# Edge stage of a graph network: TensorE's signals raised by a drain and a sequencer instruction instead of by the last matmul

## The chip, the core and the metric

The kernel runs on one core of one Trainium2 chip. The metric is device time in microseconds (us) for one execution of the whole program. Before the change it takes 3927.65 us (median of three runs, 3921.35 to 3943.58).

The engines are named as in the profile: PE (TensorE, matmuls), PEld (its weight loads), DVE (VectorE), ACT (ScalarE), POOL (GpSimd) and SP (SyncE). [...]

## The reference, cut to what matters

Four layers run one after the other on x of 8192 nodes by 128 features: a dense graph attention (`L0_gnn`), a mixture of four experts whose gates come from a sparse graph attention (`L0_ffn`), another dense graph attention (`L1_gnn`) and a second mixture of experts (`L1_ffn`). The change touches the second one alone:

```python
h = (x_flat @ W_gat).reshape(M, HEADS, NUM_EXPERTS)          # 4 heads, 4 experts
e = leaky_relu(a_src[src] + a_dst[dst], negative_slope=0.2)   # one row per edge
ee = exp(e - e_max[dst])
denom = segment_sum(ee, dst)
agg = segment_sum(h[src] * (ee / denom[dst])[:, :, None], dst)
...
for ei in range(NUM_EXPERTS):                                 # dense: every expert on every node
    hh = gelu(x @ W1[ei] + b1[ei])
    out = out + g[..., None] * (hh @ W2[ei] + b2[ei])
```

524288 edges are given, and a self loop is added for every node.

## The kernel before, in words

The stage is the block `edges` of the function `edge_gates` (from line 1023). It does two things at once: the sparse sums over the edges, and the four dense experts on all nodes. An earlier stage has sorted the edges into records, so that each of 128 partitions holds the edges of its own nodes.

**The loop.** Work goes in chunks of 16 columns of records (`CK = 16`). Four chunks (`RG = 4`, counted by `g`) make one round, and here there are five rounds: 20 chunks. In the first four rounds (`LEAD = 4`, so 16 chunks) every chunk also carries one slab of 512 nodes through the four experts. The last round has edges alone. Below, "the first 16 chunks" and "the last four chunks" mean these two loops.

**What one chunk does, by engine.**

- SP (line 1088) loads the records of a chunk into `RC[g]`, as soon as DVE has counted `gt_read` for the chunk four places earlier.
- POOL (line 1134) then issues 16 indirect DMAs, each of which gathers 128 rows of the table `tab` into `GT[g]`. Below, these 16 are called a burst.
- PE turns one-hot matrices (`look_up`, line 1362, two groups of eight transposes into `TB`, each raising `turned`), ACT copies them to `OHT` (line 1282), and PE multiplies them with `near` (line 1370, 16 matmuls into `LK`, raising `lk_ok`).
- DVE waits for `lk_ok` (line 1220), reduces `LK` (line 1221), forms the logits (lines 1223 to 1231), builds the one-hots of the next chunk (line 1152), waits for ACT's exponential (line 1287), multiplies (line 1238, after which it counts `gt_read`) and splits the values into three bf16 parts `VP` (to line 1244).
- PE scatters them (`scatter`, line 1380, 16 matmuls, raising `sc_ok`), and DVE adds the sums up (lines 1161 and 1162).
- For each expert e of the slab, PE runs `hidden` (line 1340: two matmuls of 512 columns in fp32, each recorded as two, raising `h_ok` after each), ACT applies gelu (line 1293, raising `hid_ok`), PE runs `output` (line 1348 for the bias, line 1351 for 8 matmuls, recorded as 16, raising `y_ok`), and ACT copies the result (line 1300, raising `y_used`) and sends it off (line 1303).

**The order on PE** is written out by hand: hidden(0), look_up, hidden(1), output(0), hidden(2), output(1), hidden(3), output(2), scatter, output(3). Each engine works through its own list in order, so an instruction that waits holds up all that stands behind it. Between engines there are only semaphores. A wait is followed by an increment of a semaphore `passed`, on which nobody waits; the two become one sequencer instruction.

**What PE signals, and how.** Five semaphores go from PE to the others: `h_ok` (8 per chunk of the first 16), `y_ok` (4), `turned` (2), `lk_ok` (1) and `sc_ok` (1), together 16. Each is raised by the last matmul of its group (`.then_inc`), on its completion. Signals of the sequencers, such as DVE's `gt_read`, `z_ok` and `vp_ok`, are raised by `sem_inc`, an instruction of the sequencer itself.

Of the kernel before, what the change touches and what calls it, by code (L numbers as in the profile page):

```python
# [18 lines left out]
P = 128  # L19
# [916 lines left out]
def edge_gates(nc, ident, rec, tab, tab_out, rows, ctl, repeat, b_gat, ln_gamma, ln_beta, G, XT, W1, b1, W2, b2, y, YB, y_in):  # L936
# [9 lines left out]
    NH = HE // NE  # L946
    T = N // P
    VW = NH + HE
    CK = 16
# [3 lines left out]
    D, HID = W1.shape[1], W1.shape[2]  # L953
    K = HID // P
    NG = N // BANK
    GQ = BANK // P
    NB2 = 3
    LEAD = NG // RG
    HK = CK // 2
    a_src, a_dst = rows[:, :, HE:HE + NH], rows[:, :, HE + NH:TW]  # L960
    assert HID == K * P and K == 2 and NE == 4 and RG == 4 and LEAD == 4
    with Phase(nc, "gat") as ph:
        near = ph.sbuf("near", [P, T, 3 * NH], BF16)
# [10 lines left out]
        with Phase(nc, "pre") as pp:  # L974
# [6 lines left out]
            dve_step, ext_ok, turned, diag_ok, all_ok = pp.sems("dve_step", "ext_ok", "turned", "diag_ok", "all_ok")  # L981
            with nc.Block() as block:
                @block.sync
                def _(sp):
                    sp.dma_start(RC[0][:], rv[:, 0:CK, :]).then_inc(rc_in[0], 16)
# [37 lines left out]
        with Phase(nc, "edges") as pr:  # L1023
            GT = [pr.sbuf(f"GT{k}", [P, CK, TW]) for k in range(RG)]
            node_no = pr.sbuf("node_no", [P, P])
            identB = pr.sbuf("identB", [P, P], BF16)
            OH = [pr.sbuf(f"OH{k}", [P, CK, P], BF16) for k in range(RG)]
            OHT = pr.sbuf("OHT", [P, CK, P], BF16)
            VP = pr.sbuf("VP", [P, CK, 3, VW], BF16)
# [18 lines left out]
            down = pr.sbuf("down", [P, NE, K, D])  # L1048
# [4 lines left out]
            HH = [[YB[0][:, b * K + k, :] for k in range(K)] for b in range(2)]  # L1053
            YS = [YB[1][:, e, :] for e in range(NE)]
            HP = pr.psum("hp", [P, K, BANK])
            YP = pr.psum("yp", [P, BANK])
            TB = [pr.psum(f"tb{h}", [P, HK * P], BF16) for h in range(2)]
            LK = pr.psum("lk", [P, BANK])
            OUT = [pr.psum(f"out{h}", [P, BANK]) for h in range(2)]
# [22 lines left out]
            with nc.Block() as block:  # L1082
# [250 lines left out]

                @block.tensor
                def _(pe):
                    def hidden(u, e):
                        for k in range(K):
                            pe.wait_ge(hid_ok, u * K + k + 1)
                            pe.sem_inc(passed, 1)
                            nc.tensor.matmul(HP[:, k, :], up[:, e, k * P:(k + 1) * P], XT[:, bass.ds(slab[0] * GQ, GQ), :],  # L1340
                                             start=True, stop=True).then_inc(h_ok, 1)

                    def output(u, e):
                        pe.wait_ge(hid_ok, u * K + 2 * K)
                        pe.sem_inc(passed, 1)
                        pe.wait_ge(y_used, u + 1)
                        pe.sem_inc(passed, 1)
                        nc.tensor.matmul(YP[:], oneB[0:NB2 * 32, :], b2s[0:NB2 * 32, e, :, :], start=True, stop=False)
                        for q in range(GQ):
                            for k in range(K):  # L1350
                                ins = nc.tensor.matmul(YP[:, q * D:(q + 1) * D], HH[e % 2][k][:, q * P:(q + 1) * P],  # L1351
                                                       down[:, e, k, :], start=False, stop=(q == GQ - 1 and k == K - 1))
                        ins.then_inc(y_ok, 1)

                    def look_up(k, g):
                        pe.wait_ge(oh_ok, k + 1)
                        pe.sem_inc(passed, 1)
                        for h in range(2):
                            pe.wait_ge(oht_ok, k * 2 + h + 1)
                            pe.sem_inc(passed, 1)  # L1360
                            for c in range(HK):
                                ins = nc.tensor.transpose(TB[h][:, c * P:(c + 1) * P], OH[g][:, h * HK + c, :], identB[:])
                            ins.then_inc(turned, 1)
                        pe.wait_ge(lk_read, k + 1)
                        pe.sem_inc(passed, 1)
                        for h in range(2):
                            pe.wait_ge(oht_ok, k * 2 + h + 3)
                            pe.sem_inc(passed, 1)
                            for c in range(h * HK, (h + 1) * HK):
                                ins = nc.tensor.matmul(LK[:, c * 3 * NH:(c + 1) * 3 * NH], OHT[:, c, :], near[:, g * CK + c, :], start=True, stop=True)  # L1370
                        ins.then_inc(lk_ok, 1)

                    def scatter(k, g):
                        pe.wait_ge(vp_ok, k + 1)
                        pe.sem_inc(passed, 1)
                        pe.wait_ge(acc_ok, k + 1)
                        pe.sem_inc(passed, 1)
                        for c in range(CK):
                            o = c % HK * 3 * VW
                            ins = nc.tensor.matmul(OUT[c // HK][:, o:o + 3 * VW], OH[g][:, c, :], VP[:, c, :, :].rearrange("p k v -> p (k v)"),  # L1380
                                                   start=True, stop=True)
                        ins.then_inc(sc_ok, 1)

                    rounds = rounds_of(pe)
                    pe.sem_inc(lk_ok, 1)
# [4 lines left out]
                    with pe.Fori(0, n) as l:  # L1390
                        off = begin(pe, l)
                        with pe.Fori(0, LEAD) as r:
                            for g in range(RG):
                                k, q = (off + r) * RG + g, r * RG + g
# [10 lines left out]
                        with pe.Fori(LEAD, rounds) as r:  # L1405
                            for g in range(RG):
                                k = (off + r) * RG + g
# [1482 lines left out]
```

## Time and profile before

| | us |
|---|---|
| median of three runs | 3927.65 |
| lowest, highest | 3921.35, 3943.58 |
| span of the profiled execution, first to last instruction | 3888.4 |
| median less span (start and end of the program, which the span leaves out) | 39.25 |
| edge stage, first 16 chunks (from the first `hidden` to the first matmul of the last round) | 617.6 |
| edge stage, last four chunks (to the last DVE sum) | 68.7 |

The page gives the times of one profiled execution. Its own time is not listed apart from the three; the span and the median stand 39.25 us apart. Matmul starts are recorded and their ends modelled. The name that the page gives as the releaser of a wait is inferred: where it names a transfer of an earlier stage (`sort_recs<-in_adj_dram`, `at_adj<-in_adj_dram`, `pj_Y<-in_x_dram`), the code at the waiting line says what is really waited for.

### The profile page before, as it was taken

The numbers are of one execution on the slowest core, as the hardware profiler recorded it, in microseconds if no ns is written. First come the engines' busy times: TensorE is split into PE (matmuls) and PEld (weight loads), VectorE is DVE, ScalarE is ACT, GpSimd is POOL, SyncE is SP. The second block draws the span as 40 slices with busy tenths as digits, with TensorE's granted clock in tenths as the row PEclk, the third lists the DMA queues.
The fourth block names the chain that finished last, engine by engine and source line by source line (L and its number), as shares of the span: only waits on it lengthen the run. The fifth ranks groups of instructions, "written<-read, shape, count | busy, mean of one in ns | idle before, by whom it ended". The sixth has DMA issues, their size and how long they took to land. (4 is left out here: it accounts for less than half of the span.)

```text
span 3888.4 us, 55206 instructions
## 1 busy us (share of the span) xinstructions
PE 2760.5 (71%) x16302; PEld 1676.9 (43%) x16302; DVE 2359.1 (61%) x4497; ACT 1367.3 (35%) x2278; POOL 1058.8 (27%) x1034
## 2 busy tenths in 40 slices
PE   0432127799999999994156566415899999959994
PEld 0432126644444444444044344315466566635662
DVE  9999798787878878876222222377544444343333
ACT  5310100077877878774033333214200011002221
POOL 0000100277777100000634444300012111123442
PEclk9999999999999999995577778655899999979997
DMA  5999790154645545431211112142333333314446
GB/s 203 349 383 410 303 410 22 48 194 175 218 157 189 185 168 217 154 136 44 28 39 36 33 36 38 27 163 100 96 109 108 109 105 107 104 66 129 130 126 187
DMA packets 233148, 567.74 MB, mean 146 GB/s; under 512 B 52065, under 2 KB 93384, under 8 KB 224446
## 3 DMA queue, kind: packets, MB, share of 16 engines
q1 hardware_dynamic: 145318, 375.39, 28.2%
q10 hardware_dynamic: 56152, 163.80, 11.3%
q0 software_dynamic: 31552, 27.13, 3.4%
q8 instruction: 46, 0.75, 0.1%
q14 instruction: 80, 0.66, 0.1%
HBM read 442.65 MB, written 125.39 MB: 146 GB/s over the span
## 5 line engine op out<-in xcount | busy, mean ns | idle before, releaser
L1777 PE MATMUL at_out<-at_pt,top_H 128*128 128x512 f32 x2048 | 932.0, 602 | 33.4 <-ACT at_agg L1629 29.8
L1619 ACT ACTIVATE at_rl<-at_qrow,at_less,at_steep 128x512 f32<-128x512 f32 x1024 | 742.2, 804 | 88.9 <-DVE at_pt L1705 45.4
L1705 DVE SCALAR_TENSOR_TENSOR at_pt<-at_rl,at_turned 128x1024 f32<-128x1024 f32 x512 | 626.5, 1224 | 157.2 <-PE at_out L1777 80.3
L1994 PE MATMUL at_out<-at_parts,at_a 128*128 128x387 bf16 x4096 | 688.2, 329 | 20.6 <-DVE at_parts L2067 15.7
L1777 PEld LDWEIGHTS at_out<-at_pt,top_H 128*128 128x128 f32 x2048 | 373.1, 190 | 437.8 <-issue 394.8
L1994 PEld LDWEIGHTS at_out<-at_parts,at_a 128*128 128x128 fp8e4 x4096 | 399.6, 98 | 296.1 <-issue 26.3
L896 POOL DMA_INDIRECT rec<-at_part x304 | 383.0, 1260 | 104.6 <-issue 89.0
L1134 POOL DMA_INDIRECT edges_GT<-tab,gat_RC x320 | 313.2, 979 | 335.2 <-DMA gat_RC<-rec 234.6
L1942 POOL DMA_INDIRECT slots<-at_Y,at_dest x128 | 123.3, 963 | 641.9 <-DVEq L2172 605.8
L1340 PE MATMUL edges_hp<-top_H,edges_up 128*128 x256 | 171.8, 803 | 148.7 <-issue 76.2
L645 PE MATMUL pack_bp<-top_weights,sort_recs 128*128 128x8 bf16 x1696 | 75.9, 170 | 234.7 <-DMA sort_recs<-in_adj_dram 234.7
L1221 DVE TENSOR_REDUCE edges_adv<-edges_lk 128x64 f32<-128x192 f32 x20 | 7.2, 358 | 349.1 <-DMA sort_recs<-in_adj_dram 345.1
L2445 PE MATMUL ex_hp<-ex_XS,ex_WB 128*128 128x512 f32 (+1 forms) x472 | 217.2, 597 | 1.8 <-DMA ex_WB<-wts 1.8
L2551 POOL DMA_INDIRECT y<-ex_YS,ex_to x156 | 153.3, 983 | 199.8 <-DVE ex_YS L2532 162.2
L2029 ACT ACTIVATE at_small<-at_small 128x4 f32<-128x4 f32 x16 | 3.3, 205 | 535.8 <-DVEq L2125 535.8
L2511 DVE TENSOR_TENSOR ex_HH<-ex_SU,ex_hp 128x512 f32<-128x512 f32 (+1 forms) x118 | 80.9, 686 | 162.2 <-ACT ex_SU L2489 121.5
L1293 ACT ACTIVATE f_YB<-edges_hp,edges_b1col 128x512 f32<-128x512 f32 x128 | 81.7, 684 | 251.6 <-DMA at_adj<-in_adj_dram 214.8
L645 PEld LDWEIGHTS pack_bp<-top_weights,sort_recs 128*128 128x128 fp8e4 x1696 | 61.8, 106 | 250.0 <-DMA sort_recs<-in_adj_dram 141.7
L1120 POOL IOTA edges_node_no<- 128x128 f32 x1 | 0.2, 238 | 574.0 <-POOLq L60 574.0
L1351 PEld LDWEIGHTS edges_yp<-edges_down,f_YB 128*128 128x128 f32 x1024 | 142.5, 214 | 30.8 <-issue 27.7
L2489 ACT ACTIVATE ex_SU<-ex_hp 128x512 f32<-128x512 f32 (+1 forms) x118 | 70.3, 595 | 235.1 <-PE ex_hp L2445 185.9
L1696 DVE TENSOR_SCALAR at_turned<-at_packed 128x512 uint16<-128x512 uint16 x520 | 148.0, 286 | 0.0
(543 smaller groups left out, 3745.2 us busy)
## 6 DMA issues: line engine op xcount, KB each, us to landing
sort_recs<-in_adj_dram SPq DMA_DIRECT2D x212, 512.0 KB, 8.9
at_adj<-in_adj_dram SPq DMA_DIRECT2D x192, 512.0 KB
adjT<-at_turned ACTq DMA_DIRECT2D x64, 1024.0 KB
at_a<-adjT SPq DMA_DIRECT2D x128, 512.0 KB
bucket_raw<-in_adj_dram ACTq DMA_DIRECT2D x120, 512.0 KB, 10.2
ex_WB<-wts SPq DMA_DIRECT2D x42, 533.0 KB
y<-f_YB ACTq DMA_DIRECT2D x64, 256.0 KB, 2.8
f_YB<-y SPq DMA_DIRECT2D x16, 1024.0 KB, 11.0
```

The source lines that it names most:

```text
L645: ins = nc.tensor.matmul(BP[:, u % 2, o:o + WORDS // 4], raw_bits[s % NR][:, k * P:(k + 1) * P, 0], weights[:], start=True, stop=True)
L896: pool.indirect_dma_start(rec, bass.IndirectOffsetOnAxis(ap=part[h][:, c, 2:3], axis=0), part[h][:, c, 0:2], None, bounds_check=LAST, oob_ ...
L1134: pool.indirect_dma_start(GT[g][:, c, :], None, tab, bass.IndirectOffsetOnAxis(ap=RC[g][:, c, 1:2], axis=0)).then_inc(gt_in[g], 16)
L1340: nc.tensor.matmul(HP[:, k, :], up[:, e, k * P:(k + 1) * P], XT[:, bass.ds(slab[0] * GQ, GQ), :], start=True, stop=True).then_inc(h_ok, 1)
L1351: ins = nc.tensor.matmul(YP[:, q * D:(q + 1) * D], HH[e % 2][k][:, q * P:(q + 1) * P], down[:, e, k, :], start=False, stop=(q == GQ - 1 an ...
L1619: ins = nc.scalar.activation(RL[v % NBUF][:, k, :], qrow[:], ACT.Relu, bias=less[:], scale=steep[:, u:u + 1])
L1696: ins = nc.vector.tensor_scalar(planes[m % 2][:, :, :, b, :], PK[:, m * JP:(m + 1) * JP, :].rearrange("p j (t w) -> p j t w", t=RT), b, 0x ...
L1705: nc.vector.scalar_tensor_tensor(out=PT[v % NBUF][:], in0=RL[v % NBUF][:], scalar=1.0, in1=AT[v // VP % 2][:, 2 * (v % VP):2 * (v % VP) + ...
L1777: ins = nc.tensor.matmul(OUT[:], H[:, u, :], PT[v % NBUF][:, k, :], start=(u == 0), stop=(u == T - 1))
L1994: ins = nc.tensor.matmul(OUT[:, g, x, 0:3 * D1], ones[c % NBUF][:, j, x * P:(x + 1) * P], parts[:, u].rearrange("p k d -> p (k d)"), start ...
L2445: ins = nc.tensor.matmul(HP[0:n, k, s, :], WB[b][:, w:w + n], XS[b][:], start=True, stop=True)
L2551: pool.indirect_dma_start(y, bass.IndirectOffsetOnAxis(ap=to[b][:, q:q + 1], axis=0), YS[b][:, q, :], None, bounds_check=2 * N - 1, oob_is ...
```

## The change

A helper `done` is added to the TensorE program of the block: it issues a drain, an instruction with which the sequencer waits until its engine has finished what was issued to it, and then a `sem_inc`. The five places that raised a semaphore with the last matmul of a group call it instead. No matmul, no wait and no other engine's program changes.

```diff
+                    def done(sem):
+                        nc.tensor.drain()
+                        pe.sem_inc(sem, 1)
+
                     def hidden(u, e):
                         for k in range(K):
                             pe.wait_ge(hid_ok, u * K + k + 1)
                             pe.sem_inc(passed, 1)
                             nc.tensor.matmul(HP[:, k, :], up[:, e, k * P:(k + 1) * P], XT[:, bass.ds(slab[0] * GQ, GQ), :],
-                                             start=True, stop=True).then_inc(h_ok, 1)
+                                             start=True, stop=True)
+                            done(h_ok)
...
-                        ins.then_inc(y_ok, 1)
+                        done(y_ok)
...
-                            ins.then_inc(turned, 1)
+                            done(turned)
...
-                        ins.then_inc(lk_ok, 1)
+                        done(lk_ok)
...
-                        ins.then_inc(sc_ok, 1)
+                        done(sc_ok)
```

## Rows read from the trace of the kernel before

**Rows 1.** The page: span, and TensorE's granted clock (tenths) in 40 slices.
```profile
span 3888.4 us, 55206 instructions
...
PEclk9999999999999999995577778655899999979997
```
**Rows 2.** Waits from 1868 to 2560: who waited for whom; total us, times, longest.
```profile
DVE edges_adv L1221 <- DMA sort_recs<-in_adj_dram: 345.1, 17, 53.5
POOL edges_GT L1134 <- DMA gat_RC<-rec: 234.6, 16, 17.5
...
DVE edges_adv L1221 <- PE edges_lk L1370: 4.0, 3, 1.3
```
**Rows 3.** Timeline of one chunk: start, us, engine, line, op, [idle before, releaser].
```profile
2208.04 1.88 PE L1340 MATMUL edges_hp<-top_H,edges_up 128*128 x4
...
2212.62 1.01 ACT L1282 COPY edges_OHT<-edges_tb 128x1024 bf16<-128x1024 bf16 x1
...
2214.70 1.01 ACT L1282 COPY edges_OHT<-edges_tb 128x1024 bf16<-128x1024 bf16 x1 [1.06 <-DMA pj_Y<-in_x_dram]
...
2215.86 0.36 PE L1370 MATMUL edges_lk<-gat_near,edges_OHT 128*128 128x12 bf16 x8 [1.74 <-ACT edges_OHT L1282]
...
2216.11 3.52 PE L1340 MATMUL edges_hp<-top_H,edges_up 128*128 x4
...
2219.69 1.95 PE L1351 MATMUL edges_yp<-edges_down,f_YB 128*128 128x128 f32 x16
...
2226.30 0.95 POOL L1134 DMA_INDIRECT edges_GT<-tab,gat_RC  x1 [0.30 <-issue]
2230.24 0.36 DVE L1221 TENSOR_REDUCE edges_adv<-edges_lk 128x64 f32<-128x192 f32 x1 [22.43 <-DMA sort_recs<-in_adj_dram]
2230.26 1.26 ACT L1293 ACTIVATE f_YB<-edges_hp,edges_b1col 128x512 f32<-128x512 f32 x2 [14.55 <-DMA at_adj<-in_adj_dram]
...
2231.09 3.75 PE L1340 MATMUL edges_hp<-top_H,edges_up 128*128 x4 [9.46 <-ACT f_YB L1293]
...
2244.27 1.02 PE L1340 MATMUL edges_hp<-top_H,edges_up 128*128 x2
```
**Rows 4.** Windows: stretch, length, busy of PE, PEld, DVE, ACT, POOL, granted clock.
```profile
1891.00:1895.00 4.00, 3.91 (x13) 1.69 (x14) 0.00 (x0) 0.00 (x0) 3.08 (x4) 0.50 0.13 9
1895.00:1901.80 6.80, 2.32 (x17) 2.00 (x16) 0.00 (x0) 0.00 (x0) 4.97 (x7) 1.00 0.11 9
```
**Rows 5.** Drains on PE's sequencer at a phase's end, with the matmuls before each.
```profile
2552.05 0.95 PE L1380 MATMUL edges_out<-edges_VP,edges_OH 128*128 128x60 bf16 x16 [8.70 <-DVEq L1245]
...
L1082 PEldq DRAIN  x1: 485/485/485, 2552.6 to 2552.6; - x1
...
3832.65 2.84 PE L2480 MATMUL ex_yp<-ex_WB,ex_HH 128*128 128x128 f32 x24
...
L2394 PEldq DRAIN  x1: 1968/1968/1968, 3833.6 to 3833.6; - x1
```
**Rows 6.** Lines by source: count, ns min/median/max, first to last start.
```profile
L1340 PE MATMUL edges_hp<-top_H,edges_up x256: 592/595/1217, 1868.9 to 2481.0; 128*128 x128
...
L1339 PEldq EVENT_SEMAPHORE  x128: 51/51/51, 1868.7 to 2479.1; - x128
```
**Rows 7.** Timeline: both ends of the first 16 chunks, and the look-up after them.
```profile
1868.94 3.78 PE L1340 MATMUL edges_hp<-top_H,edges_up 128*128 x4 [16.91 <-issue]
...
2486.51 1.06 PE L1362 MATMUL edges_tb<-edges_identB,edges_OH 128*128 128x128 bf16 x16
...
2493.34 0.36 PE L1370 MATMUL edges_lk<-gat_near,edges_OHT 128*128 128x12 bf16 x8 [1.96 <-issue]
...
2504.22 0.36 DVE L1221 TENSOR_REDUCE edges_adv<-edges_lk 128x64 f32<-128x192 f32 x1 [17.89 <-DMA sort_recs<-in_adj_dram]
```
**Rows 8.** Timeline, PE alone, in the first long burst.
```profile
1898.23 0.27 PE L1351 MATMUL edges_yp<-edges_down,f_YB 128*128 128x128 f32 x1 [1.45 <-issue]
1900.35 0.27 PE L1351 MATMUL edges_yp<-edges_down,f_YB 128*128 128x128 f32 x1 [1.84 <-issue]
1903.13 0.37 PE L1351 MATMUL edges_yp<-edges_down,f_YB 128*128 128x128 f32 x1 [2.52 <-issue]
```

More of the change, by code:

```diff
@@ L1350, in output @@
                             for k in range(K):
-                                ins = nc.tensor.matmul(YP[:, q * D:(q + 1) * D], HH[e % 2][k][:, q * P:(q + 1) * P],
-                                                       down[:, e, k, :], start=False, stop=(q == GQ - 1 and k == K - 1))
-                        ins.then_inc(y_ok, 1)
+                                nc.tensor.matmul(YP[:, q * D:(q + 1) * D], HH[e % 2][k][:, q * P:(q + 1) * P],
+                                                 down[:, e, k, :], start=False, stop=(q == GQ - 1 and k == K - 1))
+                        done(y_ok)
                     def look_up(k, g):
@@ L1361, in look_up @@
                             for c in range(HK):
-                                ins = nc.tensor.transpose(TB[h][:, c * P:(c + 1) * P], OH[g][:, h * HK + c, :], identB[:])
-                            ins.then_inc(turned, 1)
+                                nc.tensor.transpose(TB[h][:, c * P:(c + 1) * P], OH[g][:, h * HK + c, :], identB[:])
+                            done(turned)
                         pe.wait_ge(lk_read, k + 1)
@@ L1369, in look_up @@
                             for c in range(h * HK, (h + 1) * HK):
-                                ins = nc.tensor.matmul(LK[:, c * 3 * NH:(c + 1) * 3 * NH], OHT[:, c, :], near[:, g * CK + c, :], start=True, stop=True)
-                        ins.then_inc(lk_ok, 1)
+                                nc.tensor.matmul(LK[:, c * 3 * NH:(c + 1) * 3 * NH], OHT[:, c, :], near[:, g * CK + c, :], start=True, stop=True)
+                        done(lk_ok)
                     def scatter(k, g):
@@ L1379, in scatter @@
                             o = c % HK * 3 * VW
-                            ins = nc.tensor.matmul(OUT[c // HK][:, o:o + 3 * VW], OH[g][:, c, :], VP[:, c, :, :].rearrange("p k v -> p (k v)"),
-                                                   start=True, stop=True)
-                        ins.then_inc(sc_ok, 1)
+                            nc.tensor.matmul(OUT[c // HK][:, o:o + 3 * VW], OH[g][:, c, :], VP[:, c, :, :].rearrange("p k v -> p (k v)"),
+                                             start=True, stop=True)
+                        done(sc_ok)
                     rounds = rounds_of(pe)
```

## The prediction

> **What bounds the kernel now.** I read the page's span and clock first, then the waits inside the edge stage, then the timeline of one chunk, and last the rows of drains, of which the trace has a few elsewhere. The span is 3888.4 us and the clock of TensorE drops in the stage [rows 1]. The median of the runs, 3927.65, stands 39.25 above the span; I carry that over and count differences alone.
>
> The first 16 chunks run from 1868.94 to 2486.51 [rows 7], 617.6 us or 38.6 a chunk. No engine is full there. The waits say who is late: DVE waits 345.1 us in 17 places in front of line 1221 [rows 2]. The named releaser is a transfer of a stage long past; by the code that wait is for `lk_ok`, PE's signal that the look-up is done.
>
> The chunk shows it [rows 3]. The last look-up group starts at 2215.86 and takes 0.36, so it is done at 2216.22. DVE, idle for 22.43 us, starts at 2230.24: `lk_ok` came 14.0 us after the matmul that raises it. ACT waits for `h_ok` until 2230.26, though the `hidden` group of 2216.11 was over at 2219.63. Both came 3.9 us after POOL's last gather of the burst was issued, at 2226.30. One `turned` was late as well: ACT's second copy begins at 2214.70 and not at 2213.63, when the first was over. With POOL idle nothing of the kind happens: in the last three chunks DVE waits 4.0 us in all, 1.3 at most [rows 2]. I call this the hold: signals that PE's matmuls raise come late while a burst of gathers runs.
>
> ACT's signals don't suffer. In the same burst ACT's copy ends at 2215.71 and PE starts the look-up that waits for it at 2215.86 [rows 3], 0.15 later. [...]
>
> So the hold costs, in this chunk, PE's 9.46 us in front of the `hidden` at 2231.09 and 1.07 at ACT's copy, 10.5 of the 36.23 from 2208.04 to 2244.27 [rows 3]. POOL is no bound: a burst is 16 x (0.95 + 0.30) = 20.0 us, and it waits 234.6 us for records [rows 2], which follow DVE.
>
> **The change part by part.** *Removed:* five `.then_inc`, 16 signals in each of the first 16 chunks. If a drain ends with the matmuls and the sequencer's increment gets out, the hold goes. The trace has no drain inside a burst of gathers. Two rows at the ends of phases: one drain runs to 2552.6 + 0.485 = 2553.1, the last matmul to 2553.00; another to 3835.6, the matmuls to 3835.49 [rows 5]. Both end within 0.1 us of the work, the second amid POOL's indirect stores. I take it that a drain in a burst does so too; the other case is the first rival.
>
> The chunk without the hold, from the rows of this chunk [rows 3]: 2208.04 to 2216.22 less 1.07 is 7.1; `hidden` and `output` from 2216.22 to 2221.64 is 5.4 (at the low clock, left so); from the next `hidden` at 2231.09 to 2244.27 is 13.2. Together 25.7.
>
> *Added:* 16 drains and 16 increments a chunk. The trace shows no drain between groups, so the price has bounds. What is lost each time: the overlap with the next group (four `hidden` matmuls of 0.595 take 1.88, so they start 0.43 apart and overlap by 0.17) [rows 3, 6]; the drain's end behind the matmul, up to 0.1; the increment, 0.05, and the next wait, 0.05, which ran ahead under the matmuls until now [rows 6]; the restart from a met wait to the matmul, 0.15. Sum 0.5. Lower end 0.2: drain, increment and wait alone. Upper end 0.8: two waits, register arithmetic for their values, the low clock. I take 0.5, the sum of the nearest rows. All 16 lie on PE. The two of `turned` are hidden by ACT's copies of 1.01 each. About two more go into PE's wait for ACT's gelu before the third `hidden`, once PE is no longer slowed there by the low clock. 12 are on the path: 6.0 us. Behind each drain stands the rest of PE's list, and for that list wait ACT (gelu, copies) and DVE (scatter).
>
> [...]
>
> *The sum:* 25.7 + 6.0 = 31.7 a chunk, above POOL's 20.0. (38.6 - 31.7) x 16 = 110 us. In the last four chunks the first hold, from 2493.70 to 2504.22 [rows 7], goes: 10.5. Their four drains each, 16 x 0.5 = 8 at most, are partly under ACT: 6. Net 4.5. Together 115: 3927.65 - 115 = 3813.
>
> Ends of this case: at 0.2 a drain a chunk takes 28.1, and 168 + 8 give 3752; at 0.8 it takes 35.3, and 53 + 0 give 3875. Its own range is 3750 to 3875.
>
> **The rivals.** *The drain is held as the signals are (slower).* What is late is PE's report that a matmul is over; if the drain waits for the report and not for the array, it ends when the signal would have come, and PE's list stands still meanwhile. For it: in the long first burst PE stalls even between matmuls that carry no signal and wait for nothing, 1.5 to 2.5 us before each of three [rows 8], so reports not passed on do reach back into the engine. Against it: the drains of [rows 5], none of them in a gather burst. Price: the `hidden` and `output` that now run inside the hold, 5.4, come after it, and the drains cost 6.0: 36.2 + 11.4 = 47.6 a chunk. 11.4 x 16 = 182; 3927.65 + 182 = 4110. It decides as soon as the drains cost more than the 10.5 a chunk that the hold takes. [...] No drain here lies in a burst, so no row tests it.
>
> *The signals get out, but PE fills up (slower).* The same stalls [rows 8] say that PE takes in only so many matmuls while reports are held. DVE and ACT would get on, PE would stop one `output` later and wait for the end of the burst. It gains the 0.85 from DVE's release to the `hidden` (2230.24 to 2231.09) [rows 3] and the 1.07 at ACT's copy, and pays 6.0: 4.1 a chunk, 66 in all, 3990.
>
> *The gain is eaten (no change).* PE's short pauses at each drain lower its clock through the chunk: `hidden` matmuls of up to 1.2 instead of 0.595 [rows 6]. A `hidden` of four takes 3.75 for 1.88 [rows 3]; the two that run at the full clock now would add 3.7, and the four `output` groups some 2, an estimate from the same ratio on the part of their 1.95 that isn't yet slow: 31.7 + 5.7 = 37.4, a gain of 19 and 3909.
>
> **How the numbers follow.** The chance of the forecast is 0.48: the row of 0.15 for ACT, the clock and the drains speak for it. The held drain gets 0.25, the full PE 0.15, the eaten gain 0.12. A measurement of this kernel can tell about 0.5%, some 20 us, from no change. Faster is the forecast, 0.48; same is the eaten gain, 0.12; slower the other two, 0.40. The likeliest time is 3813. For 8 in 10 the range starts at the forecast's low end, 3750, and must reach into the held drain: to 4100, which leaves out its upper half and little at the bottom.
>
> **What would show each step.** If right: `PEldq DRAIN` rows of line `done` inside the bursts end with the matmuls; DVE's waits before line 1221 fall from 345 us to some 20 to 60; PE's 9.46 before the third `hidden` goes; the first 16 chunks take about 500 us; POOL's waits for records shrink. If the drain is held, its rows are 5 to 14 us long in each burst and PE's next weight load stands behind them. If PE fills up, the drains are short, and matmuls that wait for nothing sit idle before them. The eaten gain shows as a granted clock near 0.5 through the stage. Wrong sizes would show in the start-to-start distance of two `hidden` groups: 0.93 (0.43 + 0.5) from one group's last start by my price.

## The result, and the profile after

The changed kernel takes 4053.61 us (median of four runs, 4046.76 to 4056.15); the kernel before, on the same chip, 3933.39 (3921.35 to 3943.58). The ratio is 1.0297, 95% interval 1.0259 to 1.0335: about 120 us slower. The forecast was 3813. The kernel before took 3885.5 to 3933.4 us by chip (medians of the six groups of runs here), so every kernel below is given as a ratio to runs of the kernel before on its own chip.

The page of the changed kernel, its span and TensorE's granted clock, against [rows 1]:

```profile
span 4054.3 us, 55478 instructions
...
PEclk9999999899999999975677777755699999988997
```

That execution's time was 4056.15, so a span and its time lie 1.85 us apart, and 1.6 to 2.1 in every later run. The 39.25 us between span and median of the kernel before, which the table ahead of the prediction puts down to the program's start and end, were another thing: the profiled execution (3888.4) was faster than the three timed ones.

The stage, by the same two marks as in [rows 7] (first `hidden`, first transposes of the last round):

```profile
1884.39 1.21 PE L1344 MATMUL edges_hp<-top_H,edges_up 128*128 x1 [16.91 <-issue]
...
2653.11 1.01 PE L1367 MATMUL edges_tb<-edges_identB,edges_OH 128*128 128x128 bf16 x8 [6.51 <-issue]
```

The first 16 chunks take 768.7 us for 617.6, 48.0 a chunk for 38.6. The last four, to DVE's last sum, take 66.1 for 68.7. The stage began 15.5 us later; its start lay between 1866.6 and 1888.3 in the profiles of all the kernels of this case, and the change touches nothing ahead of it. Behind it 1.9 more went. Together: 151.1 - 2.6 + 15.5 + 1.9 = 165.9, the difference of the two spans. The cost is in the first 16 chunks.

The medians, all from one chip, differ by 120.2 and not by 165.9, since the profiled execution of the kernel before was a faster one. With the 15.5 ahead of the stage taken off, some 30 us are left that the change didn't cost. There is one profile of the kernel before, so where they lie isn't shown; every figure below that sets this profile's 768.7 beside its 617.6 can be too high by as much.

Who waited for whom, from 1868 to 2760, as in [rows 2] (the drain is at line 1337 of the changed kernel; a "q", as in PEq, PEldq and DVEq, is the profile's mark for an engine's sequencer: PEldq has the drains, semaphore instructions, 51 ns at line 1339 [rows 6], and register instructions, `ALU_OP` of 32 ns at line 1338 of the kernel before):

```profile
DVE edges_adv L1221 <- PEq L1337: 390.1, 20, 56.5
POOL edges_GT L1134 <- DMA gat_RC<-rec: 376.5, 16, 25.7
ACT f_YB L1300 <- PEq L1337: 238.9, 46, 15.2
ACT f_YB L1293 <- PEq L1337: 194.0, 81, 49.4
DVE edges_red L1161 <- PEq L1337: 118.5, 19, 8.4
ACT edges_OHT L1282 <- PEq L1337: 102.2, 37, 14.4
```

DVE's 345 us at line 1221 [rows 2] did not fall. They are 390, and now the profile names what they wait for: PE's sequencer, at the drain. POOL's waits for records rose from 234.6 to 376.5: POOL follows DVE.

One chunk, with the columns of [rows 3]:

```profile
2205.39 1.95 PE L1356 MATMUL edges_yp<-edges_down,f_YB 128*128 128x128 f32 x16
...
2214.14 0.58 ACT L1300 COPY f_YB<-edges_yp 128x512 f32<-128x512 f32 x1 [10.61 <-PEq L1337]
...
2214.48 2.07 PE L1344 MATMUL edges_hp<-top_H,edges_up 128*128 x2 [7.14 <-issue]
...
2220.12 0.61 PE L1367 MATMUL edges_tb<-edges_identB,edges_OH 128*128 128x128 bf16 x8 [1.34 <-issue]
2220.70 0.95 POOL L1134 DMA_INDIRECT edges_GT<-tab,gat_RC  x1 [0.30 <-issue]
2224.68 1.01 ACT L1282 COPY edges_OHT<-edges_tb 128x1024 bf16<-128x1024 bf16 x1 [4.30 <-PEq L1337]
...
2224.86 1.01 PE L1367 MATMUL edges_tb<-edges_identB,edges_OH 128*128 128x128 bf16 x8 [4.13 <-issue]
...
2227.70 0.36 DVE L1221 TENSOR_REDUCE edges_adv<-edges_lk 128x64 f32<-128x192 f32 x1 [20.88 <-PEq L1337]
```

The `output` group of 2205.39 is over at 2207.34. Its copy on ACT starts at 2214.14, and PE itself does nothing until 2214.48: 7.14 us in which the engine is idle and its list stands. The transposes of 2220.12 are over at 2220.73; the next eight, which need nothing but ACT's earlier copies, start 4.13 us later. POOL's last gather was issued at 2220.70; from 2224.7 on all runs freely.

The drains of line 1337: all, then one behind that `output` group, one behind a look-up in the long first burst, and one behind an `output` group with no gather about (ns: min/median/max; first and last start):

```profile
L1337 PEldq DRAIN  x272: 182/1988/42078, 1884.4 to 2716.1; - x136
...
L1337 PEldq DRAIN  x1: 8657/8657/8657, 2205.3 to 2205.3; - x1
...
L1337 PEldq DRAIN  x1: 42078/42078/42078, 1909.0 to 1909.0; - x1
...
L1337 PEldq DRAIN  x1: 2095/2095/2095, 2232.9 to 2232.9; - x1
```

The last of these lines runs from 2232.9 to 2235.0, the matmuls of that group to 2234.95: it ends with them. The one behind the `output` group of 2205.39 runs to 2214.0, 6.6 us behind its matmuls. Of all 272, 210 end within 0.05 us of their last matmul's modelled end. 59 end more than 0.5 us behind it, 244.7 us in all. Each of these 59 belongs to matmuls that ended less than 4 us after POOL had issued a gather; 100 drains do, and of the other 172 none is late. Behind the first gather of a burst (counted anew after a pause of 2 us) none of 18 drains is late; behind the second 14 of 18 are, by 0.9 to 3.3 us. The one of 42.08 us stands here, in the timeline:

```profile
1908.94 0.36 PE L1375 MATMUL edges_lk<-gat_near,edges_OHT 128*128 128x12 bf16 x8 [0.47 <-ACT edges_OHT L1282]
...
1951.21 0.36 DVE L1221 TENSOR_REDUCE edges_adv<-edges_lk 128x64 f32<-128x192 f32 x1 [56.53 <-PEq L1337]
...
1951.38 2.04 PE L1344 MATMUL edges_hp<-top_H,edges_up 128*128 x2 [42.08 <-issue]
```

Eight small matmuls over at 1909.30, and nothing more from PE for 42 us. In the kernel before, the signal of that look-up was 41.2 us late as well. There PE went on for one `hidden` and one `output` group, up to the last matmul of [rows 8], and then stood still too:

```profile
1939.77 2.05 PE L1340 MATMUL edges_hp<-top_H,edges_up 128*128 x2 [36.27 <-issue]
```

### The profile page after: what moved, and what is told of

Same layout as the page of the kernel before. It is cut to its first block and busy times, and to the rows that moved or that the text cites. A ratio compares the mean times of both kernels' runs of the same rounds, so it can differ in the third digit from the quotient of the medians.

```text
span 4054.3 us, 55478 instructions
## 1 busy us (share of the span) xinstructions
PE 2830.4 (70%) x16302; PEld 1686.9 (42%) x16302; DVE 2358.1 (58%) x4497; ACT 1375.4 (34%) x2278; POOL 1061.7 (26%) x1034
## 3 DMA queue, kind: packets, MB, share of 16 engines
q0 software_dynamic: 31552, 27.13, 3.1%
## 5 line engine op out<-in xcount | busy, mean ns | idle before, releaser
L1134 POOL DMA_INDIRECT edges_GT<-tab,gat_RC x320 | 308.8, 965 | 477.0 <-DMA gat_RC<-rec 376.5
L1344 PE MATMUL edges_hp<-top_H,edges_up 128*128 x256 | 194.8, 853 | 196.3 <-issue 191.2
L1344 PEld LDWEIGHTS edges_hp<-top_H,edges_up 128*128 128x128 f32 x256 | 50.1, 245 | 279.3 <-issue 279.3
L1356 PEld LDWEIGHTS edges_yp<-edges_down,f_YB 128*128 128x128 f32 x1024 | 151.2, 227 | 2.7
L1356 PE MATMUL edges_yp<-edges_down,f_YB 128*128 128x128 f32 x1024 | 151.2, 311 | 0.0
```

The lines of the kernel that those rows point to most:

```text
L1134: pool.indirect_dma_start(GT[g][:, c, :], None, tab, bass.IndirectOffsetOnAxis(ap=RC[g][:, c, 1:2], axis=0)).then_inc(gt_in[g], 16)
```

## The experiments

"Late" below is DVE's start at line 1221 (or the line that it has become) less the end of the last look-up matmul; 0.15 is the least that occurs.

**e1: the drains alone.** The signals stay on the matmuls, a drain stands behind each.

```diff
                                              start=True, stop=True).then_inc(h_ok, 1)
+                            nc.tensor.drain()
...
                         ins.then_inc(y_ok, 1)
+                        nc.tensor.drain()
...
```

> The kernel before with the five completions left on the matmuls, and a drain added behind each of them; no sequencer increment signals anything. Theory H (the drain is held as the completions are; the increment costs next to nothing): the signals reach the others as early as in the kernel before, yet PE's list stands at each drain in a burst of gathers, so the time is that of the changed kernel within 20 us, 4030 to 4070, and drain rows of 5 us and more stand in the bursts. Rival S (drains are short, it is the increment behind them that comes out late): drain rows end with the matmuls everywhere, and only the drains' own price is left, 12 on the path x 0.2 to 0.5 us x 16 chunks: 3970 to 4030. Rival N (the signals of the kernel before are what is late, so keeping them keeps its time): within 20 us of 3933.

Measured: 1.0361 (1.0334 to 1.0388), 4033.2 against 3889.8; first 16 chunks 758.0. The slowdown is all there with no sequencer increment. The drains behind `output` (line 1355 here):

```profile
L1355 PEldq DRAIN  x64: 2055/2122/8683, 1949.3 to 2621.0; - x64
```

Up to 8.7 us, as long as the one shown above for the changed kernel, whose longest behind an `output` group is 12.2. Theory H holds. Rival S, that the increment comes late, falls; so does rival N.

**e2 and e3: one gather a chunk.** In the kernel before (e2) and in the changed one (e3), 15 of the 16 gathers of a chunk are left out, and their columns of `GT` hold ones.

```diff
-                                for c in range(CK):
+                                for c in range(1):
                                     pool.indirect_dma_start(GT[g][:, c, :], None, tab,
...
-                                dve.wait_ge(gt_in[g], (off + r) * (16 * CK) + 16 * CK)
+                                dve.wait_ge(gt_in[g], (off + r) * 16 + 16)
```

> The kernel before with one gather in each chunk instead of 16 (the other 15 columns of GT are filled with ones once; the gathered rows of 15 of 16 columns are left out of the sums, so the gates differ). Theory H (the hold belongs to the bursts of gathers and costs about 10.5 of a chunk's 36 to 39 us): DVE's 345 us before line 1221 fall under 60, the first 16 chunks take 26 to 29 us each, and the time falls by 130 to 210 us, to 3720 to 3800. Rival L (PE's signals are late for a reason of PE's own, its queue or the fp32 matmuls, and the gathers only happen to lie there): the waits stay above 250 us and the time moves by less than 50 us, 3880 to 3940.

> The changed kernel with the same one gather in each chunk (15 of 16 columns left out as in e2). It gives the price of 16 drains a chunk where nothing is held. Theory H: drains end with the matmuls in every row, and the kernel is slower than e2 by 12 x 0.3 to 0.5 us a chunk, 58 to 96 us over 16 chunks and at most 8 in the last four. Rival P (the drains cost their own price alone and the hold has no part in the 120 us): slower than e2 by the same 110 to 145 us as between the two whole kernels. Rival C (short pauses of PE lower its granted clock and that is what costs): the granted clock of the stage falls by 0.05 or more against e2 and hidden matmuls of 1.0 us and more become the most of them.

Measured: e2 0.9329 (0.9307 to 0.9352), 258 us under before and so more than was expected. DVE still waits 102.8 us at that line in e2, not under 60, but no longer for a late signal. And e3 0.9600 (0.9577 to 0.9624), 102.2 us above e2, at the upper end of theory H. The first 16 chunks of e2 (length, busy of PE, PEld, DVE, ACT, POOL with counts, granted clock, DMA share, GB/s):

```profile
1868.30:2240.40 372.10, 300.45 (x2112) 212.89 (x2113) 147.79 (x332) 199.21 (x277) 19.26 (x19) 0.94 0.13 46
```

The same of e3:

```profile
1867.80:2335.90 468.10, 349.73 (x2112) 210.81 (x2113) 147.77 (x332) 206.25 (x278) 18.68 (x19) 0.91 0.10 37
```

Without bursts the kernel before needs 23.3 us a chunk and not 38.6, at a granted clock of 0.94. The bursts cost it 617.6 - 372.1 = 245.5 us. (e2's span is 259.3 under that of the kernel before, its median 258.4, so here the profiles agree with the medians.) In e2 the look-up's signal is 0.15 late in every chunk but the first (0.36), as here, where its last matmul is over at 2109.32:

```profile
2108.98 0.34 PE L1375 MATMUL edges_lk<-gat_near,edges_OHT 128*128 128x12 bf16 x8 [0.57 <-ACT edges_OHT L1287]
...
2109.47 0.36 DVE L1226 TENSOR_REDUCE edges_adv<-edges_lk 128x64 f32<-128x192 f32 x1 [5.78 <-PE edges_lk L1375]
```

e3 is 96.0 us longer than e2 over these 16 chunks, 6.0 a chunk: the price of the drains where nothing is held. All 272 of them end within 0.03 us of their matmuls. Their length:

```profile
L1342 PEldq DRAIN  x272: 184/1075/3948, 1867.9 to 2391.9; - x136
```

The longest, 3.9 us from 2142.33, is the length of the `output` group with its bias that starts at 2142.26; the granted clock was 0.50 there. By the profiled executions the changed kernel's 768.7 are thus 372.1 of work, 96.0 of drains and 300.6 for the bursts, 55 more than the bursts cost before, of which some 30 are in doubt, as said above.

Rival P (the drains' own price is the whole loss) isn't excluded by this pair alone: 102.2 us by the medians stand beside 120.2 for the whole change, and P asked for 110 to 145. So the larger part of what was *added* is the drains' own price, and the hold was there already. What speaks against P are the late drains shown above, and e1: on the chip of e2 and e3 it costs 143.4 us, 41 more than the drains cost where nothing is held. Rival C (the clock) has little: 0.94 to 0.91, inside the 96.0.

**e12 and e18: half of the change each.** e12 has drain and increment for `turned`, `lk_ok` and `sc_ok`; e18 for `h_ok` and `y_ok`.

```diff
-                            ins.then_inc(turned, 1)
+                            done(turned)
...
-                        ins.then_inc(lk_ok, 1)
+                        done(lk_ok)
...
-                        ins.then_inc(sc_ok, 1)
+                        done(sc_ok)
```

> Half of the change: drain and increment for turned, lk_ok and sc_ok only (4 of 16 signals a chunk, one group of look-up and the scatter), h_ok and y_ok left on their matmuls. Theory H (what costs is PE's list standing at a drain in a burst; the look-up lies in the burst in most chunks): at least half of the slowdown with a quarter of the drains, 1.015 to 1.03 of before. Rival P (each drain costs the same): a quarter of it, 1.005 to 1.01. If these signals came out sooner by the drain and freed DVE: under 1.00.

> The other half of the change on the kernel before, at its full pace of gathers: drain and increment for h_ok and y_ok (12 of 16 signals a chunk), the look-up's and the scatter's left on their matmuls. e12, the other half, gave 1.010, the whole 1.030. Theory H (a drain costs by where it lies in a burst, not by its kind): 1.01 to 1.03, with drain rows of 4 us and more behind hidden and output groups in the bursts. If the halves add up: 1.02. If one long wait takes the place of another, whichever drain is there: 1.025 to 1.035 with this half alone.

Measured: e12 1.0099 (1.0082 to 1.0116), e18 1.0355 (1.0325 to 1.0386). The 12 drains of the dense experts make the whole slowdown, and the halves don't add up; that is nearest to the third expectation of e18, that one long wait takes the place of another. The drains behind `hidden` and `output` stop the list ahead of the look-up. With a quarter of the drains e12 pays a third, less than theory H wanted and within rival P's 1.005 to 1.01; but by P the 12 drains of e18 would give about 1.022. Nor is the time that drains are held their cost: e12's end 288 us behind their matmuls in all, e18's 164, and yet e18 costs over three times as much. The longest drain of e18 is the hold of the first burst again:

```profile
L1337 PEldq DRAIN  x192: 1073/2023/48860, 1880.2 to 2628.6; - x192
```

**e4, e9, e5 and e6: two, three, four and eight gathers under way.** This is the kernel before, except that POOL waits, before each gather, until the one so many places earlier in its burst has landed. The edit for two:

```diff
                                 for c in range(CK):
+                                    if c >= 2:
+                                        pool.wait_ge(gt_in[g][c % 2], (off + r) * (CK // 2 * 16) + c // 2 * 16)
+                                        pool.sem_inc(passed, 1)
                                     pool.indirect_dma_start(GT[g][:, c, :], None, tab,
```

> The kernel before, with POOL waiting before each gather until the one two places earlier has landed, so at most two are under way. Theory Q (signals are held behind a queue of gathers that are not landed yet; POOL issues one every 1.25 us and signals come 3.9 us after the last issue): with two under way a signal is late by one landing at most, 2 to 4 us, DVE's waits at line 1221 fall from 345 to under 150 us; a burst takes 16 x 1.25 to 2 = 20 to 32 us, and the time is 3820 to 3930. Rival G (signals are held as long as POOL goes on issuing gathers, however few are under way): the bursts get longer, the hold with them, DVE's waits rise above 400 us and the time is 4000 to 4150.

> The kernel before, at most four gathers under way. With two there was no hold (DVE's reduction of line 1221 stood 0.15 us behind the last look-up matmul in every chunk but the first), but POOL issued a gather only each 1.80 us and a chunk took its 16 x 1.8 to 1.9 = 30 us. Theory Q (the hold grows with the gathers that are under way, and four are still few): the gather period comes back to 1.3 us, a chunk falls to PE's own 23 to 26 us, and the time is 0.94 to 0.96 of before. Rival T4 (the hold is there as soon as the gathers are issued at full rate, whatever their number): lk_ok late by 4 us and more again in most chunks, 0.97 to 1.00 of before.

> The kernel before, at most eight gathers under way. Theory Q: between four and no limit; the signal of the look-up is late by a few us, at most the landing of eight gathers, 8 x 1.25 = 10; 0.95 to 1.00 of before. If a burst of 16 at 1.25 us each never has eight under way, the limit never binds and it is the kernel before, within 0.5%.

> The kernel before, at most three gathers under way: between two (no hold, one gather each 1.80 us, 0.980 of before) and four (hold of 8 to 14 us in half the chunks, one each 1.26 us, 1.009). Theory R (the hold comes with the rate: a gather takes the chip some 1.3 to 1.5 us beyond the queue, and at one each 1.26 us the work behind POOL piles up): three let the queue fill, the median period is under 1.4 us and the hold is back in many chunks, 0.98 to 1.01. Theory C (it comes with the count, from the fourth on): no look-up signal late by over 1 us, period 1.3 to 1.5, a chunk 24 us, 0.94 to 0.96.

Measured: two 0.9799 (0.9778 to 0.9821), three 1.0016 (0.9988 to 1.0043), four 1.0087 (1.0054 to 1.0119), eight 1.0077 (1.0054 to 1.0100). With two under way the look-up's signal is never over 0.34 late, and the kernel is faster than the kernel before and the changed one:

```profile
2119.23 0.95 POOL L1137 DMA_INDIRECT edges_GT<-tab,gat_RC  x1 [0.33 <-issue]
...
2121.02 0.95 POOL L1137 DMA_INDIRECT edges_GT<-tab,gat_RC  x1 [0.84 <-DMA edges_GT<-tab,gat_RC]
2121.18 0.36 PE L1374 MATMUL edges_lk<-gat_near,edges_OHT 128*128 128x12 bf16 x8 [0.56 <-ACT edges_OHT L1286]
...
2121.68 0.36 DVE L1224 TENSOR_REDUCE edges_adv<-edges_lk 128x64 f32<-128x192 f32 x1 [7.14 <-PE edges_lk L1374]
```

Amid gathers DVE starts at 2121.68, as soon as it ever does after the look-up's end at 2121.54. But POOL issues one gather each 1.80 us (median) and bounds the chunk at 30.2. With three and four the median time from one gather to the next is 1.26 again and the hold is back; in this chunk of the kernel with four (look-up over at 2128.14) the signal is 11.9 late:

```profile
2127.78 0.36 PE L1374 MATMUL edges_lk<-gat_near,edges_OHT 128*128 128x12 bf16 x8 [4.65 <-ACT edges_OHT L1286]
...
2140.05 0.36 DVE L1224 TENSOR_REDUCE edges_adv<-edges_lk 128x64 f32<-128x192 f32 x1 [22.15 <-DMA sort_recs<-in_adj_dram]
```

So theory Q was wrong as it stood: the time doesn't fall as the queue gets shorter from 16 to three, and with four and eight it is longer than any of the expectations had it. The largest lateness does fall (42.6 us with eight, 14.3 with four, 12.7 with three), so the length of the queue has some part in it. Either the count from three on or the pace decides.

**e8: plain loads.** Each gather is replaced by a load of 128 rows in order, from the same table to the same place, issued by POOL; the gather by index is left out.

```diff
-                                    pool.indirect_dma_start(GT[g][:, c, :], None, tab,
-                                                            bass.IndirectOffsetOnAxis(ap=RC[g][:, c, 1:2], axis=0)).then_inc(gt_in[g], 16)
+                                    pool.dma_start(GT[g][:, c, :], tab[c * P:(c + 1) * P, :]).then_inc(gt_in[g], 16)
```

> The kernel before with each gather replaced by a plain load of 128 rows of the same table to the same place (rows in order and not by the records' indices, so the gates differ), issued by POOL as before. Theory W (the hold comes from many small writes into SBUF, whoever makes them): DVE's waits before line 1221 stay above 250 us, time within 2% of before. [...]

Measured: 3638.3 (one run), against 3908.5, 270 less; first 16 chunks 372.5, as with one gather. One load is issued each 0.54 us, and the look-up's signal is 0.15 late while they run:

```profile
2107.24 8.61 POOL L1134 DMA_DIRECT2D edges_GT<-tab  x16 [13.44 <-DMA gat_RC<-rec]
...
2113.89 0.34 PE L1369 MATMUL edges_lk<-gat_near,edges_OHT 128*128 128x12 bf16 x8 [0.57 <-ACT edges_OHT L1281]
...
2114.38 0.36 DVE L1220 TENSOR_REDUCE edges_adv<-edges_lk 128x64 f32<-128x192 f32 x1 [5.78 <-PE edges_lk L1369]
```

On its page the queue of POOL's transfers moved as many packets and bytes as in the changed kernel (31552 and 27.13 MB on both pages):

```profile
q0 software_dynamic: 31552, 27.13, 2.9%
```

So it isn't the many small writes into SBUF (theory W). It is something of the indirect form, or of the order of the rows: these loads read the table's rows one after the other, and the two weren't tried apart.

**e10, e11 and e13 to e16: the pace of the gathers.** These have no limit on the gathers under way; POOL clears a small tile behind each. In e10 and e11 it waits for the clearing itself, which made the pace slower than aimed at (1.97 and 2.18 us, not 1.5 and 1.75). In e13 to e16 it waits for the clearing two places back; the tiles have 32, 160, 288 and 384 columns. In e13 to e15 the pace came out faster than aimed at. The edit of e13 to e16:

```diff
+                                    pool.wait_ge(paced, (off + r) * (RG * CK) + g * CK + c + 1)
+                                    pool.sem_inc(passed, 1)
+                                    nc.gpsimd.memset(idle[:, c % 2, :], 0.0).then_inc(paced, 1)
```

> The kernel before, no limit on the gathers under way, but POOL clears a small tile behind each gather and waits for it, so a gather is issued each 1.5 us or so instead of 1.26. Theory R (rate): the pile no longer grows, or hardly; look-up signals late by under 2 us, a chunk takes POOL's 16 x 1.5 = 24 us, 0.94 to 0.97 of before. Theory C (count of gathers under way): as a gather needs some 3 us, two to three are under way at this pace and there is no hold either; only a landing time over 4 us would keep it. Rival G (any gather being issued holds the signals until POOL stops): the hold lasts as long as the burst, now 24 us of a longer chunk, 1.02 to 1.06.

> As e10 with a larger tile, one gather each 1.7 to 1.8 us, the pace that two in flight had by itself. If the pace alone does it (theories R and C), no signal is late and the time is that of e4, 0.975 to 0.985 of before, as POOL's 16 x 1.75 = 28 us bound the chunk. Rival (the waits of POOL do it, which stop its sequencer between two gathers, and not the pace): the hold of 10 us and more stays, 1.00 to 1.06.

> The kernel before, no limit on gathers under way, POOL clears a tiny tile (32 columns) behind each gather; it waits only for the clearing two places back. Theory R (the hold comes when gathers are issued faster than the chip works them off, somewhere between one each 1.26 us, held, and one each 1.80 us, not held): period 1.35 to 1.55 us; if that is slow enough, look-up signals come 0.15 us behind the last matmul, a chunk takes 24 to 27 us, 0.94 to 0.97 of before. If the border lies above: hold of 4 us and more in many chunks, 0.98 to 1.01. Rival (POOL's waits on other engines' or DMA's events break the hold, not the pace): hold as in the kernel before, 0.99 to 1.01, at any period.

> As e13 with 160 columns: period 1.5 to 1.7 us. Theory R: no hold, POOL's 16 x 1.6 and one stall of 2 us bound the chunk at 26 to 29 us, 0.95 to 0.975 of before. Rival: hold as before, 0.99 to 1.03.

> As e13 with 288 columns: period 1.6 to 1.85 us. Theory R: no hold, a chunk of 28 to 32 us, 0.965 to 0.99 of before, above e14 by 16 to 20 chunks x 16 x the difference of the periods. Rival: hold as before, 1.00 to 1.05.

> As e15 with 384 columns: period 1.57 to 1.60 us. At 1.26, 1.37 and 1.48 the look-up signal came up to 15, 5 to 9 and 2 us late. Theory R: at 1.58 it comes under 0.5 us late in most chunks; a chunk takes between PE's own 23.3 and POOL's 16 x 1.58 + 2 = 27.3 us, and the time is 0.945 to 0.965 of before. If the shorter hold is eaten by POOL's longer bursts: 0.96 to 0.98.

Measured (period: median time from one gather to the next; 16 periods: what POOL needs for a chunk at that pace; late: the look-up's largest of the 20 chunks; all us):

| kernel | period | 16 periods | a chunk, first 16 | late | ratio to before (95%) |
|---|---|---|---|---|---|
| before | 1.26 | 20.2 | 38.6 | 41.2 | 1 |
| e13 | 1.26 | 20.2 | 42.2 | 15.5 | 1.0158 (1.0126 to 1.0191) |
| e14 | 1.37 | 21.9 | 36.0 | 9.2 | 0.9905 (0.9871 to 0.9939) |
| e15 | 1.48 | 23.7 | 30.3 | 2.9 | 0.9639 (0.9616 to 0.9661) |
| e16 | 1.56 | 25.0 | 27.0 | 1.1 | 0.9586 (0.9565 to 0.9608) |
| e4 (two under way) | 1.80 | 28.8 | 30.2 | 0.3 | 0.9799 (0.9778 to 0.9821) |
| e10 | 1.97 | 31.5 | 34.2 | 0.4 | 0.9917 (0.9901 to 0.9934) |
| e11 | 2.18 | 34.9 | 37.3 | 0.4 | 1.0082 (1.0053 to 1.0112) |

Two bounds cross here. From 1.26 to 1.56 the hold melts away; from 1.56 on POOL's own 16 periods, and some 2 us of stalls, are the chunk. e13 has the same added instructions as e16, on a smaller tile, and the hold, so it isn't POOL's waiting or clearing as such that ends it, but the time between gathers. (Why e13 is slower than the kernel before at the same period isn't shown.) e11's time lies in its rival's range, but without a hold: its pace alone made it slow. In e14 the hold is smaller but still there, and its time lies above theory R's range. e14, with two gathers 1.37 apart; look-up over at 2097.01, 7.0 late:

```profile
2094.90 0.96 POOL L1137 DMA_INDIRECT edges_GT<-tab,gat_RC  x1 [0.17 <-POOL edges_idle L1141]
2096.27 0.96 POOL L1137 DMA_INDIRECT edges_GT<-tab,gat_RC  x1 [0.17 <-POOL edges_idle L1141]
2096.65 0.36 PE L1376 MATMUL edges_lk<-gat_near,edges_OHT 128*128 128x12 bf16 x8 [3.26 <-issue]
...
2104.03 0.36 DVE L1227 TENSOR_REDUCE edges_adv<-edges_lk 128x64 f32<-128x192 f32 x1 [16.79 <-DMA sort_recs<-in_adj_dram]
```

e16, 1.56 apart; over at 2104.44, 0.15 late:

```profile
2102.47 0.96 POOL L1137 DMA_INDIRECT edges_GT<-tab,gat_RC  x1 [0.17 <-POOL edges_idle L1141]
...
2104.03 0.96 POOL L1137 DMA_INDIRECT edges_GT<-tab,gat_RC  x1 [0.17 <-POOL edges_idle L1141]
2104.08 0.36 PE L1376 MATMUL edges_lk<-gat_near,edges_OHT 128*128 128x12 bf16 x8 [0.55 <-ACT edges_OHT L1288]
...
2104.59 0.36 DVE L1227 TENSOR_REDUCE edges_adv<-edges_lk 128x64 f32<-128x192 f32 x1 [7.85 <-PE edges_lk L1376]
```

e16 has the lowest ratio of the kernels that do all the work: 3746.8 against 3906.9, 4.1% under the kernel before.

**e7 and e17: the change where nothing is held.** The changed kernel with at most two gathers under way (e7, the edit of e4) and at the pace of e16 (e17).

> The changed kernel, at most two gathers under way. Theory H (drains are held only where completions are held): no drain row ends over 0.5 us behind its last matmul, and the change costs against e4 only its own price: the stage is bound by POOL at 30 us a chunk in e4 and the drains fit under it in part, so 0.98 to 1.00 of the kernel before, 0 to 2% above e4. Rival P (the drains cost the full 120 to 150 us whatever the gathers do): 1.01 to 1.02 of the kernel before.

> The changed kernel at the same pace as e16, all gathers done. Theory H: drains end with their matmuls (late by under 1 us), and the change costs what its 16 drains cost by themselves and no more: a chunk of 29 to 31 us as with few gathers (e3: 29.25), so 30 to 90 us above e16, 0.96 to 0.985 of before, and faster than the kernel before. Rival P (the change costs its 120 to 150 us whatever the gathers do): 0.98 to 1.00.

Measured: e7 0.9755 (0.9711 to 0.9798), e17 0.9607 (0.9582 to 0.9631). e7 is no slower against its own chip than e4; 27 of its 272 drains still end over 0.5 us behind their matmuls, 2.4 at most, where none was expected. Beside e16, on the same chip, e17 is 8 us longer, not 30 to 90, and their intervals overlap. Its drains:

```profile
L1343 PEldq DRAIN  x272: 182/1073/3933, 1885.8 to 2424.4; - x136
```

The 42 and 8.7 us are gone, with every gather in its place: 4 drains end over 0.5 us behind their matmuls, none over 1.0. The drains' own price is still paid, 48.6 us in the first 16 chunks (480.1 for 431.5), and given back in the last four (61.7 for 102.7), since POOL's 320 gathers bound both kernels. So this pair shows the drains short, and not what they would cost if POOL left room. In e16 they run from 1868.9 to 2398.0:

```profile
L1137 POOL DMA_INDIRECT edges_GT<-tab,gat_RC x320: 957/957/3025, 1868.9 to 2398.0; - x160
```

And in e17 from 1877.1 to 2405.4, 528.3 us for 529.1:

```profile
L1137 POOL DMA_INDIRECT edges_GT<-tab,gat_RC x320: 957/961/3081, 1877.1 to 2405.4; - x160
```

## Why the prediction was wrong, point by point

*What bounds the kernel: right, and undersized.* The signals of PE are late in bursts of gathers, and that is what the stage loses. The term was 10.5 of 36.2 us a chunk; e2 makes it 15.3 of 38.6. The chunk without the hold was put together at 25.7 and is 23.3: the low clock of `hidden` and `output` was "left so", and in e2 it goes too (granted clock of the first 16 chunks 0.94, in the kernel before 0.77). The matmuls themselves weren't late: 13 are recorded in the 4.00 us from 1891.00, in a burst [rows 4], while DVE got its signal of that look-up at 1932.66. "The clock", as a ground for the chance of 0.48, was the author's inference: the granted clock was 0.50 in those 4.00 us and 1.00 in the next 6.80, and no run shows that this tells when the engine worked.

*The drain ends with the matmuls: the step that failed.* The whole gain of the sum hung on it: 12.9 a chunk (38.6 less 25.7) over 16 chunks and 10.5 behind them, 217 us. Without that gain the same sum comes to 102 us slower; 120 were measured. The step rested on the two drains of [rows 5]. Neither lay in a burst of gathers, as the text said, and the second lay amid indirect stores, which was taken as near enough. In a burst a drain is held as the completion is: 59 of the changed kernel's drains, 42.08 us at most. e1 shows that this is the drain's doing and not the increment's, e17 that it ends when the gathers are slowed. The rows that stood against the step, PE's own stalls in the long burst [rows 8], were rows of a burst and should have outweighed rows of another place. In e1, which has both, the completion of the first burst's look-up is 41.1 us late and the drain behind it 42.4: the drain isn't ahead of the completion.

*The price of a drain: right.* It was to be 12 on the path at 0.5, 6.0 a chunk; e3 less e2 gives 6.0. The distance from a `hidden` group's last start to the next group's was to be 0.93. In e3:

```profile
2110.24 1.10 PE L1349 MATMUL edges_hp<-top_H,edges_up 128*128 x2 [0.33 <-issue]
...
2111.66 1.10 PE L1349 MATMUL edges_hp<-top_H,edges_up 128*128 x2 [0.32 <-issue]
```

The second matmul of a pair starts 1.10 - 0.595 = 0.5 after the first, so the distance is 2111.66 - 2110.74 = 0.92.

*The last four chunks: wrong term.* The first hold there was to go (10.5) and the drains to take 6. The stretch is 2.6 shorter; the hold is still there, now as 6.51 and 6.77 us in which PE stands before its two groups of transposes. The drains alone take 2.4 there (59.2 in e3, 56.8 in e2).

*The sum.* 31.7 a chunk was forecast; 48.0 came. If one knew only that the drain is held, the prediction's own rival had it: 11.4 more than before a chunk, measured 9.4 (48.0 less 38.6). Its time of 4110 was 56 too high: 33 are that term (182 against 151.1 - 2.6), and 23 are the distance from the 148.5 of the two profiled executions to the 126 between the changed kernel's median and 3927.65, which isn't the change's. The rows of the burst itself spoke for this rival, and it got 0.25.

*The other rivals.* PE didn't fill up: no drain was short with PE idle before matmuls that wait for nothing. The eaten gain wanted a lower clock, and the granted clock of the first 16 chunks did fall, from 0.77 to 0.70, and from e2 to e3 from 0.94 to 0.91; from e16 to e17, with the same drains added, it rose from 0.87 to 0.90. So it isn't shown that short pauses lower it, and no gain was there to eat.

*The 39.25.* To carry the difference of median and span over as a fixed part was wrong; time less span is 2.1 us at most.

What stays open: what a gather has in common with PE's completions. The pace decides (41.2 us late at 1.26, 1.1 at 1.56), and the number of bytes and packets doesn't (27.13 MB and 31552 with the hold and, in e8, without); the indirect form or the order of its rows matters. Indirect stores issued 1.29 us apart in runs of four, at the end of the kernel before (POOL, line 2551), hold next to nothing: DVE's start at line 2532 is 0.04 us behind the last matmul of `ex_yp` in 37 of 38 places, and 0.76 in one, each time 1 to 3 us after a store was issued. Whether longer runs would wasn't tried.

## What to carry to other kernels

Here a drain was no way round a completion that is late: it was late with it (42.4 beside 41.1 us in e1), and it stopped the engine's own list as well (7.14 us at the `output` group of 2205.39), so move a signal off the matmul only where the row of a drain in that very stretch shows it short. Before changing how a signal is raised, look at what runs while it is late; here a small clear behind each gather, 0.3 us more from one gather to the next, gave 4.1% (e16), and the change cost 3%. A row from another stretch of the kernel is weaker evidence than a weak row from the stretch itself.

## What the runs showed of the hardware

- While POOL issues indirect gathers one each 1.26 us, PE's completions and drains come late, up to 42 us in a burst of 64 (47 in e18). The look-up's signal is 9.2 us late at most at one each 1.37 (e14), 2.9 at 1.48 (e15), 1.1 at 1.56 (e16), 0.4 at 1.97 and 2.18 (e10, e11). With two gathers under way drains are still up to 2.4 us late (e7). With plain loads of as many rows at one each 0.54 us the look-up's signal is 0.35 us late at most, and mostly 0.15 (e8). PE starts 0.15 us after ACT's copy inside a burst [rows 3].
- A drain and a sequencer increment behind each of 16 groups cost 6.0 us a chunk where nothing is held (e3 less e2), though each drain there ends 0.02 us behind its matmuls' modelled end.
- Slowing an engine that isn't the bottleneck, POOL, by a quarter (1.26 to 1.56 us a gather) made the kernel faster, 0.9586 of before in e16; at 1.97 it was 0.9917 and at 2.18 1.0082, with POOL's own 16 periods, 31.5 and 34.9 us, as most of a chunk of 34.2 and 37.3.
